# Cross-attention and FFN block: where and when the tail's weights and the first heads are loaded

## The reference, cut to what matters

```python
q  = _ln(_fp8_linear(ln_out, wq)); k = _ln(_fp8_linear(ln_out, wk)); v = _fp8_linear(ln_out, wv)
core = softmax(q @ k.T / sqrt(128)) @ v                 # per group, 2 query heads
xout = the same with qx and kx, vx from ctx
catq = div_clamp_fp8(concatenate([core, xout]), proj_smooth)
x = x + (catq @ wproj.T) * (proj_in_scale * proj_w_scale)
z = layernorm(x)
x = x + down((silu(gate(z)) * up(z)))                   # W = (wq - 128) * scale, three int32 matrices
```

## Time and profile before

| | |
|---|---|
| median of three runs | 1833.42 us |
| the profiled execution | 1835.97 us |
| its span, first to last instruction | 1834.1 us |
| TensorE busy | 1655.5 us (90%) |
| ScalarE busy | 1403.9 us (77%) |
| VectorE busy | 1364.6 us (74%) |
| GpSimd busy | 1086.3 us (59%) |

### The profile page before, as it was taken

One profiled execution on the slowest core, in us unless ns is written; L12 is line 12 of the kernel. 1 busy time (PEld: TensorE's weight loads), 2 busy tenths in 40 slices (PEclk: granted clock), 3 DMA queues, 4 the chain that ended last, 5 costly groups with the idle time before them and its releaser, 6 DMA issues. The chain is left out here.

```text
span 1834.1 us, 43340 instructions
## 1 busy us (share of the span) xinstructions
PE 1655.5 (90%) x15491; PEld 1237.8 (67%) x15776; DVE 1364.6 (74%) x3172; ACT 1403.9 (77%) x2936; POOL 1086.3 (59%) x1022
## 2 busy tenths in 40 slices
PE   1459999999999999999999999999998479999999
PEld 1337788778778877887887788778776334444444
DVE  8988988997898899889879988998777432323232
ACT  6669999999999999999999999999999343031211
POOL 1147777777777777777777777777777203030202
PEclk9769999999999999999999999999999789999999
DMA  5028768978787787888778778877889980021100
GB/s 167 24 69 139 139 129 161 145 137 141 142 150 133 142 155 148 134 149 158 125 145 154 136 131 160 153 133 131 172 161 178 279 297 1 25 114 69 68 23 23
DMA packets 641005, 240.32 MB, mean 131 GB/s; under 512 B 612640, under 2 KB 612640, under 8 KB 640800
## 3 DMA queue, kind: packets, MB, share of 16 engines
q1 hardware_dynamic: 640800, 237.66, 64.1%
HBM read 65.58 MB, written 20.99 MB: 47 GB/s over the span
## 5 line engine op out<-in xcount | busy, mean ns | idle before, releaser
L971 POOL TENSOR_TENSOR local<-local 128x512 bf16<-128x512 f32 x512 | 607.2, 1186 | 339.4 <-ACT local L880 339.4
L578 PE MATMUL ps_pj<-wide 128*128 128x256 bf16 (+1 forms) x5544 | 585.2, 255 | 12.7 <-ACT local L803 10.8
L578 PEld LDWEIGHTS ps_pj<-wide 128*128 128x128 bf16 x5544 | 470.7, 98 | 125.5 <-issue 12.0
L877 ACT ACTIVATE local<-ps_s,neg_max 128x512 f32<-128x512 f32 x512 | 389.6, 761 | 46.9 <-DVE neg_max L1178 45.9
L626 PE MATMUL ps_o<-v_hi,local 128*128 128x129 bf16 x2048 | 379.9, 223 | 31.2 <-DMA local<-local 29.3
L880 ACT ACTIVATE local<-ps_s,neg_max 128x512 bf16<-128x512 f32 x512 | 392.3, 766 | 13.9 <-DMA local<-local 13.9
L1178 DVE TENSOR_REDUCE neg_max<-ps_s 128x1 f32<-128x512 f32 x512 | 345.8, 676 | 53.6 <-PE ps_s L642 51.5
L628 PE MATMUL ps_o<-v_hi,local 128*128 128x129 bf16 x2048 | 379.4, 220 | 0.0
L627 PE MATMUL ps_o<-local 128*128 128x128 bf16 x2048 | 379.1, 219 | 0.0
L803 ACT ACTIVATE local<-ps_pj,head_rstd 128x128 f32<-128x128 f32 x756 | 238.2, 434 | 44.0 <-issue 40.2
L947 POOL TENSOR_TENSOR head_rstd<-sq_sum,minus_half 128x3 f32<-128x3 f32 x256 | 218.5, 854 | 25.0 <-DVE sq_sum L1114 25.0
(11 more groups left out here) (112 smaller groups left out, 2591.6 us busy)
## 6 DMA issues: line engine op xcount, KB each, us to landing
w_raw<-w_group SPq DMA_DIRECT2D x32, 512.0 KB, 4.3
quantised_heads<-local SPq DMA_DIRECT2D x32, 512.0 KB, 3.2
wide<-quantised_heads SPq DMA_DIRECT2D x4, 4096.0 KB, 13.1
local<-local SPq DMA_TRANSPOSE x640, 3.2
wide<-x SPq DMA_DIRECT2D x8, 1024.0 KB, 11.8
local<-ctx_t SPq DMA_DIRECT2D x4, 1024.0 KB, 5.3
w_raw<-w_proj SPq DMA_DIRECT2D x8, 512.0 KB, 4.5
wide<-w_proj SPq DMA_DIRECT2D x4, 1024.0 KB, 6.1
```

What stands on the lines that cost most here:

```text
L578: last = mm(dst[:, at:at + n], lhs, w_at(par, part, c, cross * 512 + at, n), start=(k == 0), stop=(k == len(terms) - 1))
L877: a(p_exp[:, u % 2], ps_s[u % 2][:], ACT.Exp, bias=neg_max[:, u % 4:u % 4 + 1])
L971: tt_(pp[:, u % PP_BUFS, 1], p_exp[:, u % 2], pp[:, u % PP_BUFS, 0], ALU.subtract)\
```

## The change

`wide` is laid out by batch: each batch has its own region of `xq`, `ctx_hi`, `ctx_lo` (RB = 12288 bf16 columns). Batch 0's place takes half of `wp` and x, batch 1's gate and up, batch 2's `w_down` and three working tiles, batch 3's the heads; and the two places of the group's weights swap. What takes a batch's place can be written as soon as group 7 has projected that batch. The tail's weights come in 38 pieces of at most 0.5 MB through `w_raw`: 16 of `wp`, 16 of gate and up (each half a chunk, 128x704 int32), 6 of `w_down`. ScalarE issues their DMAs. The first 24 are loaded in slots 1, 3, ... 47 of group 7 and converted by VectorE two slots later; the last 14 are loaded in slots 56 to 69 and converted by ScalarE in slots 58 to 71. The heads of batch 0 come in eight pieces of 0.5 MB, issued by ScalarE in slots 48 to 55 and clipped by VectorE in slots 50 to 57. x comes in slot 40. The output projection runs in slots 51 to 72, four matmuls a slot in the slots proper and nine a slot in the drain, all four tiles. SyncE no longer issues any of these.

```diff
-        xq = carve([SETS, CH, NTOK], BF16)
-        ctx_hi = carve([CH, NTOK], BF16)
-        ctx_lo = carve([CH, NTOK], BF16)
+        for _ in range(B):
+            xq.append(carve([SETS, CH, T], BF16))
+            ctx_hi.append(carve([CH, T], BF16))
+            ctx_lo.append(carve([CH, T], BF16))
+        wp_low = carve([WP_HALF, DM], BF16)
+        wp_high = home(W_FIRST + PAR)([WP_HALF, DM], BF16)
+        wgu = home(RB)([CH, 2 * HID], BF16)
+        carve = home(2 * RB)               
+        heads_in = home(3 * RB)([G, HEADS, T], BF16)
...
-        EARLY_SLOTS = [2 + 5 * n for n in range(EARLY_PIECES)]
-        CONVERT_LAG = 3
-        STAGE_SLOTS = [SLOTS - UNITS + 2 + 2 * n for n in range(PROJ_PIECES)]
-        STAGE_SLOTS += [SLOTS + CONVERT_LAG + n for n in range(TAIL - CONVERT_LAG - 3)]
-        HEADS_SLOT = STORE_LAG + SLOTS - UNITS
-        CLIP_SLOT = HEADS_SLOT + 6
-        EARLY_TILES, EARLY_FIRST = 3, SLOTS + 3
+        CONVERT_LAG = 2
+        HEADS_SLOT = SLOTS - UNITS
+        LOAD_SLOTS = [1 + 2 * n for n in range(DVE_PIECES)]
+        LOAD_SLOTS += [HEADS_SLOT + G + n for n in range(ACT_PIECES)]
+        CONVERT_SLOTS = [slot + CONVERT_LAG for slot in LOAD_SLOTS]
+        X_SLOT = HEADS_SLOT - 8
+        CLIP_FIRST = HEADS_SLOT + 2
+        OUT_FIRST = CLIP_FIRST + 1
+        EARLY_TILES, OUT_STEP, DRAIN_STEP = 3, HEADS, 9
...
ScalarE (in a slot: convert before the two exponentials, loads behind them)
+            def load_piece(n):
+                if n == 0:
+                    act.wait_ge(w_ready, CH * G + W_FREE)
+                elif n >= DVE_PIECES + 2:
+                    act.wait_ge(conv_act, n - 1 - DVE_PIECES)
+                elif n >= 2:
+                    act.wait_ge(conv_dve, n - 1)
+                src = late_piece(n)[0]
+                act.dma_start(piece_raw(n, src), src).then_inc(piece_loaded[n % 2], 16)
+            def convert(n):
+                src, dst, offset = late_piece(n)
+                act.wait_ge(piece_loaded[n % 2], 16 * (n // 2 + 1))
+                act.wait_ge(proj_done, home_free(n))
+                a(dst, piece_raw(n, src), ACT.Copy, bias=offset).then_inc(conv_act, 1)
+            def load_heads(p):
+                if p == 0:
+                    act.wait_ge(proj_done, GROUP_TILES * G)
+                    act.wait_ge(heads_stored, 16 * (B * (G - 1) + 1 + FREE))
+                if p >= 2:
+                    act.wait_ge(heads_piece[p % 2], 16 * (p // 2))
+                act.dma_start(heads_in[:, p].rearrange("p h t -> p (h t)"), heads_dram[0, p]).then_inc(heads_piece[p % 2], 16)
...
VectorE (in a slot: behind the maximum and L1186, ahead of the quantisation)
+                    if last and CLIP_FIRST <= slot < CLIP_FIRST + G:
+                        clip_piece(slot - CLIP_FIRST)
+                    if last and slot in CONVERT_SLOTS[:DVE_PIECES]:
+                        convert(CONVERT_SLOTS.index(slot))
...
TensorE (in a slot: behind scores and head transposes, ahead of the projection)
+                    for n in out_range(slot) if last else ():
+                        tt, f = divmod(n, G * HEADS)
+                        if n == 0:
+                            pe.wait_ge(conv_dve, WP_PIECES)
+                            pe.wait_ge(qn_done, GROUP_TILES * G)
+                        if tt == 0 and f % HEADS == 0:
+                            pe.wait_ge(clipped, f // HEADS + 1)
+                        if tt == 2 and f == 0:
+                            pe.wait_ge(full_done, GROUP_TURNS * G)
+                        if tt == EARLY_TILES and f == 0:
+                            pe.wait_ge(exp_done, SLOTS * G)
+                        out_matmul(OUT_BANKS[tt], tt, f)
...
-            pe.wait_ge(stage_done, N_STAGE)
+            pe.wait_ge(conv_dve, DVE_PIECES)
+            pe.wait_ge(conv_act, ACT_PIECES)
             gate_up(0)
```

More of the change, by code:

```diff
@@ L263, in block_kernel @@
         heads_stored = sem("heads_stored")
-        stage_loaded = [sem(f"stage_loaded{i}") for i in range(2)]
-        stage_done = sem("stage_done")
-        early_done = sem("early_done")
+        piece_loaded = [sem(f"piece_loaded{i}") for i in range(2)]
+        conv_dve = sem("conv_dve")
+        conv_act = sem("conv_act")
+        heads_piece = [sem(f"heads_piece{i}") for i in range(2)]
         sdown_in = sem("sdown_in")
@@ L309, in block_kernel, with out_range, done @@
         TAIL = 4 + STORE_LAG
-        EARLY_SLOTS = [2 + 5 * n for n in range(EARLY_PIECES)]
-        CONVERT_LAG = 3
-        STAGE_SLOTS = [SLOTS - UNITS + 2 + 2 * n for n in range(PROJ_PIECES)]
-        STAGE_SLOTS += [SLOTS + CONVERT_LAG + n for n in range(TAIL - CONVERT_LAG - 3)]
-        CONVERT_SLOTS = [slot + CONVERT_LAG for slot in STAGE_SLOTS]
-        HEADS_SLOT = STORE_LAG + SLOTS - UNITS
-        CLIP_SLOT = HEADS_SLOT + 6
-        EARLY_TILES, EARLY_FIRST = 3, SLOTS + 3
-        EARLY_STEP = -(-EARLY_TILES * G * HEADS // (SLOTS + TAIL - EARLY_FIRST))
+        CONVERT_LAG = 2
[7 more added lines that the diff above has]
+        EARLY_TILES, OUT_STEP, DRAIN_STEP = 3, HEADS, 9
+        def out_range(slot):
+            def done(s):
+                if s < OUT_FIRST:
+                    return 0
+                n = OUT_STEP * (min(s, SLOTS) - OUT_FIRST) + DRAIN_STEP * max(s - SLOTS, 0)
+                return min(n, TT * G * HEADS)
+            return range(done(slot), done(slot + 1))
         def slots(last):
@@ L753, in scale_in @@
                     k = s * CH + c
[L754 removed]
+                    last = a(xq[b][:, s, c], IN_BANKS[n % len(IN_BANKS)][:], ACT.Identity,
                              scale=ln_scale[:, k:k + 1], bias=ln_bias[:, k:k + 1])
@@ L872, in group @@
                         weight_hi((g + 1) % 2, c, CH * g + CH + c + 1)
+                    if last and slot in CONVERT_SLOTS[DVE_PIECES:]:
+                        convert(CONVERT_SLOTS.index(slot))
                     for u in unit_at(slot, EXP_LAG, first):
@@ L890, in group @@
                         qk_high(q, j, GROUP_TURNS * g + 3 * (2 + q) + j)
-                    if last and slot in CONVERT_SLOTS:
-                        convert(CONVERT_SLOTS.index(slot))
             for g in range(G):
                 group(g, g == 0, g == G - 1)
-            for n in range(len(CONVERT_SLOTS), N_STAGE):
-                convert(n)
             def finish(b):
@@ L1191, in group @@
                         weight_sums(c, CH * g + CH + c + 1)
-                    if last and slot == CLIP_SLOT:
-                        clip_heads(0)
+                    if last and CLIP_FIRST <= slot < CLIP_FIRST + G:
+                        clip_piece(slot - CLIP_FIRST)
+                    if last and slot in CONVERT_SLOTS[:DVE_PIECES]:
+                        convert(CONVERT_SLOTS.index(slot))
                     for H in head_at(slot, QUANT_END_LAG, first):
```

192 lines of the change are left out of this document (83 added, 109 removed).

## The result

The changed kernel takes 1814.57 us, the median of 7 runs (1809.40 to 1823.32); the kernel before took 1831.51 beside it (7 runs, 1829.66 to 1835.13). The ratio is 0.9907, 95% interval 0.9891 to 0.9922: faster by 0.9%. The profiled execution took 1815.63 us, its span is 1813.8. Its runs lie 14 us apart, those of before 5.5.

A forecast was written before the change was run, and what follows sets the result against it. Attention was taken as bound by matmuls, TensorE and ScalarE nearly full in step, with a slower stretch behind it. 1835.97 - 31 (tail) + 14 (group 7) = 1819; that execution was 2.55 us above the median, so 1816, range 1801 to 1830.

The forecast's parts named there:

- The tail: From slot 48 to the end of the output projection: ends at 1467.0 instead of 1497.9, 31 us less.
- Slots 56 to 63: ScalarE loads and converts a piece per slot with two buffers: 3.05 us a slot, unit 63 at 1446.5, 11.6 earlier.
- the prediction's first rival: Group 7: the load-to-load chain does not bind, the whole 31 us stay less 2 for small waits: 1804 us; 27%.
- Slots 48 to 55: Heads replace 4 MB of `wp`: same bytes, same 21.0 us, plus 1 us for clips, unit 56 at 1425.7.
- the loop: Group 7's 48 slots: load, landing, conversion, quantisation, maximum, exponential, next load take 11.5 us against 10.4, twelve rounds, 11 us.
- GpSimd's exclusion: Group 7: VectorE's conversions wait up to 0.95 us beside GpSimd; taken at 0.25 a round, 12 rounds, 3 us.
- its signs: Group 7: VectorE idle for the DMA ahead of conversions in slots with s mod 4 = 1, ScalarE idle for the maximum.
- the issue of the load: Group 7: ScalarE's load stands behind its slot's second exponential, which lets go 0.57 us after its start.
- The landing: Group 7: a piece lands 4.5 us after its load is issued; bounds 3.9 and 5.4.
- the second rival: Group 7: DMA engines bind at a share of 1.04, transposes land late, TensorE waits, another 8 us: 1824; 9%.
- The third rival: Group 7: conversions at upper prices cost 3.85 us a round, twelve rounds 46 us, slower than before: 1848; 9%.
- the fourth: Group 7's buffer places are not free, so the change does not do what it says: 1833; 1%.

The follow-up runs named there:

- no_bytes_all: The changed kernel with all of ScalarE's loads (38 pieces, heads, x) carrying only a few columns, waits and conversions kept: 1799.44 us.
- no_bytes: The changed kernel with the 24 loads that VectorE converts bringing only 16 columns each, waits and conversions kept: 1812.49 us.
- small_convert: The changed kernel with VectorE converting only 16 columns of each of its 24 pieces, loads and waits kept: 1816.40 us.
- x_late: The changed kernel with the 1 MB load of x in slot 70 instead of slot 40: 1819.28 us.
- sp_loads: The changed kernel with the first 24 loads issued by SyncE, at the end of the slot behind theirs, instead of by ScalarE: 1824.83 us.
- no_bytes_late: The changed kernel with x, the heads and the last 14 pieces carrying few columns, the first 24 pieces whole: 1800.51 us.
- x62: The changed kernel with the 1 MB load of x in slot 62 instead of slot 40: 1822.74 us.

## Why the prediction was right, and where not

The time was right: 1816 us predicted, 1814.57 measured. So was the FFN's start: about 1495 predicted, 1492.3 measured. The reason was right in the main for the tail and wrong for group 7, and the closeness of the total is partly luck.

**The tail.** Slots 56 to 63 were to last 20.8 us, and lasted 22.4; the projection was to end 20.5 us behind unit 63, and did so in 20.2; the layer norm hid ScalarE's last conversions as predicted (13.6 to 13.4 us). The granted clock was 0.93 and 0.92 in slots 48 to 63 and 1.00 behind them, near full as assumed. The pace of slots 56 to 63 was not the steady 3.05 us a slot of the working: the first took 6.3 us, with ScalarE waiting for its first piece, the six behind it 2.7 each. With unit 63 at 48.5 us behind unit 48 instead of 43 and 54.3 before, the stretch from unit 48 to the FFN is 26 us shorter, not 31. The 31 us are there without the bytes, though: with few bytes in flight (no_bytes_all) the kernel takes 1799.44 us, where the prediction's first rival, the tail's gain and no loss, had 1804.

**Slots 48 to 55** were to take 22.0 us, "same bytes, so the same 21.0 us, and 1 us for the clips" (unit 56 at 1425.7, which is 0.2 more than 1403.5 and 22.0 give). They took 26.1. The bytes were not the same. SyncE's issues in the kernel before, whose unit 48 is at 1403.7 and unit 56 at 1424.8 (each of these loads is 1 MB of `wp`, and between the two shown stands one more, at 1412.47):

```profile
1406.60 0.57 SPq L447 DMA_DIRECT2D wide<-w_proj  x1
...
1418.94 0.57 SPq L447 DMA_DIRECT2D wide<-w_proj  x1
...
1425.17 0.58 SPq L447 DMA_DIRECT2D wide<-w_proj  x1
```

Three of the four fall into these slots, so 3 MB were replaced by 4 MB of heads; by the rates above, 236 GB/s over 21.0 us and 260 over 26.0, 5.0 MB moved there before and 6.8 after, transposes included. Loads left over from the slots ahead explain 2 us of it at most: with the early pieces emptied (no_bytes) the share is still 1.18 and the stretch 24.0 us. Without the late bytes it takes 20.5, clips included, so the clips cost little; no run is without them.

**Group 7.** The step that failed is the loop: "from load to load, four slots: 11.5 us", in which VectorE waits for its piece. It was priced at 11 us, with GpSimd's exclusion 14. Its place in the sum (138 us for 48 slots) was off by 6, since they took 132.0, and its signs, VectorE idle ahead of its conversion and ScalarE for the maximum, did not come: they waited 3.1 and 3.4 us in all. The input that was wrong is the issue of the load: "it stands behind the second exponential ... and lets go 0.57 later". It is issued 2.0 us ahead of that in ten rounds of twelve. The landing held (median 4.2 to 4.3, not 4.5). VectorE's conversion did not: it took 1.33 us in the median and up to 1.49, where I had 0.81 for 1024 columns and 0.65 for 704, and GpSimd's exclusion, priced at 0.25 a round, is most of the difference (1.31 us for 704 columns while GpSimd worked, 0.53 while it was idle, both rows below). These longer conversions push quantisation and maximum back without any wait for a piece: 2.0 us in twelve slots by small_convert. With ScalarE's eight conversions gone, what is left is 2 us in 48 slots (126.3 in no_bytes_all, 126.5 in x_late, against 124.5). sp_loads shows the loop binding: with the load 2.8 us later the 48 slots cost 9 us more. That run also puts the loads in the transposes' queue, and no run took the two apart; the 26.6 us of VectorE's waits speak for the loop.

```profile
1385.28 1.31 DVE L1195 TENSOR_SCALAR wide<-w_raw 128x704 bf16<-128x704 int32 x1
...
1392.96 0.53 DVE L1195 TENSOR_SCALAR wide<-w_raw 128x704 bf16<-128x704 int32 x1 [2.06 <-DMA w_raw<-w_gate]
```

**What stands in its place** is near the second rival, which had 9%: the DMA engines. It foresaw a share of 1.04 in group 7 and late transposes; the share is 1.08, and TensorE waits 7.0 us for them. But it put the cost on the 24 early pieces, and these cost about 1 us with the late loads emptied (no_bytes_all against no_bytes_late) and no more than a few beside them (0.9903 in no_bytes, 0.9907 and 0.9915 in the change). The 15.8 us are those of the loads from slot 40 on. Of the 7.5 us that the 48 slots lost, 5.5 are gone in x_late and 2.5 in x62, where x is loaded elsewhere. I had counted the tail's bytes as unchanged and so never priced them, though the earlier trace rows had the share at 1.02 already there. So the working had 14 us for a loop that cost 2, and nothing for bytes that cost some 16. These two errors of 12 and 16 us have opposite signs, and that the total came out so close is luck. The 54% for "loop of 14 us" was too much, and the contention deserved more than 9%.

The third rival (slower, from 2.6 us a round) did not come: the 48 slots lost 7.5 us in all, not 46. Nor did the fourth, places that are not free.

## What to carry to other kernels

Before bytes are moved into a stretch, read the share of the DMA engines there. Here the 128x512 transposes landed in 3.2 us (median) at a share of 0.69 to 0.91, in 4.3 at 1.08 and in 5.9 at 1.16 to 1.20, though the other loads were in another queue; emptying the late loads gave back 12 of 48.5 us in the slots at 1.16 to 1.20, and emptying the early ones 1.5 us in the 48 slots. Take the bytes of such loads out in one experiment before anything is rearranged: that run shows in one number what is at stake (here 16 of 1816 us), and which loads are harmless. Look, too, whether an experiment that cuts an instruction short did so in the trace: 16 columns in place of 1024 left 0.88 us of 1.33. When a load's issue is part of a chain, take its time from a row of that engine's queue, not from its place in the program.

## What the runs showed of the hardware that I had not expected

- A DMA issue in ScalarE's program starts ahead of exponentials that stand before it: 0.89 us before the first of them where ScalarE was behind with its work, in the same moment where the first one waited for a semaphore (1385.14 and 1385.15), and together with the second at 1393.40, where that one waited. It takes 0.33 to 0.45 us, also where it starts while SyncE issues a transpose (1.23 us), so no wait of one for the other is seen.
- One 4 MB load issued by ScalarE holds a transpose that SyncE issues for 9.60 us, against 1.23 undisturbed.
- A VectorE conversion of 16 columns took 0.96 us where a GpSimd subtraction had started 0.23 us ahead of it (1.16 us long), and 0.18 once where GpSimd was idle; one of 704 columns took 1.31 beside GpSimd and 0.53 without.
